# Scans, small VectorE operations and Pool scatters of a gated linear attention, placed elsewhere in a round

## What is computed

```python
h = _layernorm(x) * (1 + ca) + sa                    # x: (32, 256, 128)
q, k, v = h @ W_q, h @ W_k, h @ W_v                  # 16 heads of 64
a = sigmoid(h @ W_gate + b_gate)
def step(S, qkva):                                   # over the 256 tokens
    S = a_t[..., None] * S + k_t[..., None] * v_t[..., None, :]
    return S, einsum('bhk,bhkv->bhv', q_t, S)
x = x + ga * (scan(step) @ W_o)
h = _layernorm(x) * (1 + cb) + sb
probs = sigmoid(h @ router_w.T + routing_bias)       # top 2 of 8, normalised
x = x + gb * (shared(h) + sum over the 2 chosen experts of w_e * down_e(silu(gate_e h) * up_e h))
```

## Time and profile before

| | us |
|---|---|
| median of 3 runs | 1336.66 (1334.47 to 1336.96) |
| the profiled execution's own time | 1335.02 |
| its span, first to last instruction | 1332.9 |
| PE busy | 1209.7 (91%) |
| VectorE busy | 1039.1 (78%) |
| Pool busy | 946.5 (71%) |
| ACT busy | 717.1 (54%) |

### The profile page before, as it was taken

How to read it: one execution, slowest core, us unless ns; L and a number is a source line. 1 busy time by engine, 2 the same in 40 slices (tenths; PEclk the granted TensorE clock), 3 DMA queues, 4 the chain that set the end, 5 groups by cost and what they waited for, 6 DMA issues and landing times. The chain is left out here.

```text
span 1332.9 us, 35442 instructions
## 1 busy us (share of the span) xinstructions
PE 1209.7 (91%) x10935; PEld 1063.2 (80%) x10935; DVE 1039.1 (78%) x2183; ACT 717.1 (54%) x1637; POOL 946.5 (71%) x1288
## 2 busy tenths in 40 slices
PE   5999999999999999998999999999989799999960
PEld 5888878888888878787888888887878688898850
DVE  7778788787878788888878787878766478887767
ACT  4666656556555556555555655655645345445420
POOL 4336687768696968778786969686876457777754
PEclk9999999999999999999999999999999999999995
DMA  8810202021120202020202112020202266666146
GB/s 247 240 69 2 90 22 87 25 85 58 47 98 7 101 8 97 10 95 20 85 24 85 63 42 101 4 101 8 99 26 92 70 189 193 191 178 182 61 155 224
DMA packets 88445, 119.30 MB, mean 90 GB/s; under 512 B 9652, under 2 KB 52327, under 8 KB 88384
## 3 DMA queue, kind: packets, MB, share of 16 engines
q1 hardware_dynamic: 79296, 101.47, 23.7%
q0 software_dynamic: 9088, 17.07, 3.7%
HBM read 50.29 MB, written 61.79 MB: 84 GB/s over the span
## 5 line engine op out<-in xcount | busy, mean ns | idle before, releaser
L1188 DVE TENSOR_TENSOR pairs<-qk_banks,pairs 128x512 f32<-128x512 f32 x256 | 164.5, 684 | 82.0 <-PE qk_banks L1537 81.5
L1638 PE MATMUL vo_bank<-A,shared 128*64 128x256 f32 (+1 forms) x2048 | 197.0, 335 | 27.5 <-POOL A L510 26.7
L710 POOL DMA_INDIRECT y_dram<-pairs,y_row x156 | 158.2, 1014 | 68.2 <-issue 43.9
L1176 DVE TENSOR_TENSOR_SCAN pairs<-pairs,shared 128x515 f32<-128x515 f32 x128 | 174.2, 1361 | 36.3 <-POOL pairs L593 30.1
L510 POOL TENSOR_SCALAR_AFFINE_SELECT A<-A 128x256 f32<-128x256 f32 x256 | 100.0, 416 | 136.3 <-ACT A L786 136.1
L1623 PE MATMUL score_banks<-pairs 64*128 64x128 f32 x2048 | 193.1, 286 | 3.2 <-ACT kx L779 3.2
L1638 PEld LDWEIGHTS vo_bank<-A,shared 128*64 128x64 f32 x2048 | 129.3, 138 | 81.7 <-issue 24.0
L1181 DVE TENSOR_TENSOR_SCAN pairs<-pairs,shared 128x515 f32<-128x515 f32 x128 | 167.8, 1311 | 0.0
L1623 PEld LDWEIGHTS score_banks<-pairs 64*128 64x128 f32 x2048 | 147.0, 189 | 25.7 <-issue 25.7
L584 POOL DMA_INDIRECT rows_dram<-token_rows,dest x120 | 124.9, 1041 | 58.3 <-issue 31.5
L767 ACT ACTIVATE shared<-vo_bank 128x512 f32<-128x512 f32 x128 | 76.5, 598 | 165.0 <-PE vo_bank L1638 165.0
(11 more groups left out here) (252 smaller groups left out, 3163.9 us busy)
## 6 DMA issues: line engine op xcount, KB each, us to landing
rows_dram<-pad_row SPq DMA_DIRECT2D x17, 2112.0 KB, 8.1
ga_all<-rows_dram SPq DMA_DIRECT2D x39, 264.0 KB
pairs<-y_dram SPq DMA_DIRECT2D x16, 512.0 KB
pairs<-in_L_ffn_gate_w_dram SPq DMA_DIRECT2D x39, 128.0 KB
pairs<-in_L_ffn_up_w_dram SPq DMA_DIRECT2D x39, 128.0 KB
ga_all<-in_L_ffn_down_w_dram SPq DMA_DIRECT2D x39, 128.0 KB, 2.2
mod_rows<-mod_rows_dram SPq DMA_DIRECT2D x32, 128.0 KB, 3.1
h_all<-h_tile SPq DMA_DIRECT2D x16, 256.0 KB, 2.3
```

The source lines that it names most:

```text
L710: g.indirect_dma_start(y_dram, bass.IndirectOffsetOnAxis(ap=y_row[:, u, n:n + 1], axis=0), y_out[:, u, n, :], None, bounds_check=TOKENS * ...
L1176: v.tensor_tensor_scan(G[:, 0:WIDE - 1], gi_t[:, 0:WIDE - 1], cap[:, 0:WIDE - 1], 1.0, ALU.mult, ALU.min)
L1188: v.tensor_tensor(out[:, :, :].rearrange("p u (c t) -> p u c t", c=CHUNKS), QKS[:, :, off:off + T].rearrange("p u (c t) -> p u c t", c=CHU ...
L1638: last = t.matmul(VO[h * DK:(h + 1) * DK, u * T + k * P:(u + 1) * T], v_sb[:, k, vcols], blocks.rearrange("p c t -> p (c t)"), start=(k == ...
```

## The change

Five things move, all in the written order. On VectorE the scans of a duo, which stood at the end of a step, now stand in the next step, just ahead of the products that use them. `places` is cut in two: `rank_rows`, which reads the ranks, stands ahead of the scans in step 4, `destinations` behind the products. `choose` goes from step 3 to step 2, the second normalisation is split over steps 5 and 6, `moments` go to steps 1 and 6; what stood ahead of the products (normalisation, `split_h`) now stands behind them. On Pool the eight scatters of a round go from steps 5, 6, 7, 0 in twos to 3, 2, 2, 1 in steps 5, 6, 0, 1, and both `h_rows` stand at the end of their steps.

```diff
--- before.py
+++ after.py
@@ -625,8 +625,8 @@
                     b, d = i * 2 + half, i * 2 * DUOS + s
                     if e == 0 and not (last and half == 1):
                         inverse_std(b + 2)
-                    if s == 0 and three:
-                        scatter_rows(i - 2, s_fill, (i - 2) * 16, (6, 7))
+                    if s < 2 and three:
+                        scatter_rows(i - 2, s_fill, (i - 2) * 16, ((5, 6), (7,))[s])
                     if s in (1, 2) and two:
                         for n in range(2):
                             logits_exp(i - 1, (s - 1) * 2 + n)
@@ -634,17 +634,15 @@
                         update_x(b - 1)
                     if s == 4 and one:
                         inverse_std2(i)
-                    if s == 6 and one:
-                        h_rows((i - 1) * 2 + 1, i - 1, 1, i)
-                    if s >= 5 and two:
-                        scatter_rows(i - 1, s_fill, (i - 1) * 16, ((0, 1), (2, 3), (4, 5))[s - 5])
+                    if s in (5, 6) and two:
+                        scatter_rows(i - 1, s_fill, (i - 1) * 16, ((0, 1, 2), (3, 4))[s - 5])
                     mask_second_head(d)
                     if not (last and s == 2 * DUOS - 1):
                         growth(d + 1)
                     if not (last and s >= 2 * DUOS - 2):
                         gates(d + 2)
-                    if s == 5 and one:
-                        h_rows((i - 1) * 2, i - 1, 0, i)
+                    if s in (5, 6) and one:
+                        h_rows((i - 1) * 2 + s - 5, i - 1, s - 5, i)
 
             inverse_std(1)
             pool.wait_ge(s_wsplit, 4)
@@ -660,7 +658,7 @@
             with pool.Fori(3, ROUNDS - 1) as i:
                 round_of_steps(i, False)
             round_of_steps(ROUNDS - 1, True)
-            scatter_rows(ROUNDS - 2, s_fill, (ROUNDS - 2) * 16, (6, 7))
+            scatter_rows(ROUNDS - 2, s_fill, (ROUNDS - 2) * 16, (5, 6, 7))
             update_x(B - 1)
             logits_exp(ROUNDS - 1, 0)
             inverse_std2(ROUNDS)
@@ -1147,17 +1145,20 @@
                 chosen(k, 6)
                 v.tensor_tensor(picked[:, :, :], pick[:, 0, :, :], pick[:, 1, :, :], ALU.add).then_inc(s_pick, 1)
 
-            def places(k, where=dest):
-
-                def step(count):
-                    alone(s_pl, (k - 1) * 3 + count)
+            def rank_rows(k):
 
                 alone(s_rk, k)
                 v.tensor_tensor(place_e[:, :, :], RANK[:, 0:PT * E].rearrange("p (n e) -> p n e", n=PT),
                                 next_row[:, :].rearrange("p (a e) -> p a e", a=1).broadcast_to([P, PT, E]),
                                 ALU.add).then_inc(s_pl, 1)
-                step(1)
+                alone(s_pl, (k - 1) * 3 + 1)
                 v.tensor_tensor(next_row[:, :], next_row[:, :], RANK[:, PT * E:(PT + 1) * E], ALU.add).then_inc(s_pos, 1)
+
+            def destinations(k, where=dest):
+
+                def step(count):
+                    alone(s_pl, (k - 1) * 3 + count)
+
                 for t in range(TOP):
                     ins = v.tensor_tensor(place_k[:, t, :, :], pick[:, t, :, :], place_e[:, :, :], ALU.mult)
                 ins.then_inc(s_pl, 1)
@@ -1166,6 +1167,10 @@
                 step(3)
                 alone(s_e0, k)
                 v.tensor_copy(where[:, :], place_f[:, :, :].rearrange("p t n -> p (t n)")).then_inc(s_dest, 1)
+
+            def places(k, where=dest):
+                rank_rows(k)
+                destinations(k, where)
 
             def scans(d):
 
@@ -1205,35 +1210,35 @@
                     b, d = i * 2 + half, i * 2 * DUOS + s
                     more = not (last and half == 1)
                     first_head(d)
-                    if s == 3 and two:
-                        choose(i - 1)
-                    if s == 5 and one:
-                        for u in range(2):
-                            normalise2((i - 1) * 2 + u, u, i)
+                    if s == 0 and two:
+                        logits(i - 1)
+                    if s == 4 and two:
+                        rank_rows(i - 1)
+                    if s in (5, 6) and one:
+                        normalise2((i - 1) * 2 + s - 5, s - 5, i)
+                    if not (last and s == 2 * DUOS - 1):
+                        scans(d + 1)
+                        products(d + 1)
+                    if s == 4 and two:
+                        destinations(i - 1)
                     if e == 0 and more:
                         normalise(b * CHUNKS + CHUNKS, s_rs, b + 2, s_xn)
-                    if s == 0 and two:
-                        logits(i - 1)
                     if e == 1 and more:
                         split_h((1 - half) * T, b + 2)
-                    if s == 4 and two:
-                        places(i - 1)
-                    if not (last and s == 2 * DUOS - 1):
-                        products(d + 1)
+                    if s == 2 and two:
+                        choose(i - 1)
                     if s == 3 and two:
                         weigh(i - 2, i - 1)
                     if s == 3 and one:
                         moments2(b - 1, 1, i)
                     if s == 7:
                         moments2(b - 1, 0, i + 1)
-                    if e == (3 if isinstance(b, int) and b == 0 else 2) and not last:
+                    if s == (6 if half else 3 if isinstance(b, int) and b == 0 else 1) and not last:
                         if isinstance(b, int) and b == 0:
                             dve.wait_ge(s_x_rest, 16)
                         moments(b * CHUNKS + 2 * CHUNKS, b + 3)
                     if s == 3 and not one:
                         split_shared_expert()
-                    if not (last and s >= 2 * DUOS - 2):
-                        scans(d + 2)
 
             dve.wait_ge(s_const, 15)
             v.tensor_copy(counting[:, :, :], causal[:, 0:2, :])
@@ -1242,7 +1247,6 @@
             dve.wait_ge(s_sh, 1)
             dve.wait_ge(s_x_next, 16)
             moments(CHUNKS, 2)
-            scans(1)
             for i in range(3):
                 round_of_steps(i, False)
             with dve.Fori(3, ROUNDS - 1) as i:
```

## The result

The changed kernel takes 1345.41 us (median of 6 runs, 1344.34 to 1347.52), the kernel before, on the same chip, 1336.81 (6 runs, 1334.47 to 1340.32): a ratio of 1.0065, 95% interval 1.0049 to 1.0080. It is slower by 8.6, some three times the 2.7 that the prediction took a measurement to tell; 1330.7 had been forecast, with 0.36 on slower.

What follows compares the result with a forecast made beforehand. PE bounds the kernel, busy 57.77 of 61.60 a round. At -0.6 a round, twelve loop rounds give -7.2, rounds 2 and 15 -1.2, rounds 0 and 1 +2.4: -6.0, to 1330.7; range 1296 to 1367.

Steps and rivals of the forecast that it cites:

- A chain exactly as long as PE's work: Each step: scores, first-head masking, scans, products, key copy, next scores take 6.93 against PE's 6.91, so nothing more is hidden.
- A select costs a scan 0.13: Where scans meet Pool's mask: one select lengthens a scan by 0.13, with bounds 0 and 0.39.
- case (i): Mask begun before the first scan: scans lose 0.05 + 0.13, the step is scans' end + 1.74; taken for steps 0, 3, 4.
- The rival of the full hold: Each select costs a scan 0.39, +0.95 a round over 14 rounds, 1355 in all; 12 in 100.
- case (ii): Mask begun in the first scan: scans lose 0.13, step is scans' end + 1.87; taken for steps 2, 6, 7.
- the 8.0 in brackets: Step 1: its length if the second power falls behind a scan, given beside the forecast 7.6.
- case (iii): Mask begun in the second scan: no scan loses, mask ends 0.56 behind, step is scans' end + 2.25; steps 1, 5.
- Step 5, three scatters of 1.40 each, mask near 5.2: Step 5: first scatter 0.92 after the destinations, then 1.40 each, mask near 5.2; step length 8.05, +0.91.
- Rounds 0 and 1, +2.4: Early rounds without routed work or stall to lose: their twelve 6.91 steps become 7.1, +2.4 in all.
- scans and selects do not hinder each other: Rival: step lengths are the larger of chain and PE, -2.6 a round, 1300 in all; 20 in 100.
- the mask behind both scans: Rival: Pool's mask lies behind both scans in every step, +1.75 a round over 14 rounds, 1367; 18 in 100.
- the last rival: PE alone: chain and mask hidden, all 4.2 a round gone, 1278 in all; 5 in 100.

Runs made afterwards that it cites:

- E5: The changed kernel without Pool's causal mask of the second head (its two selects in every step), ScalarE scaling that head's scores by 1e-20; 1291.61, ratio 0.9659.
- E12: The changed kernel with the whole place computation of step 4 ahead of the scans, so destinations come sooner; 1337.56, ratio 1.0003 to the kernel before.
- E6: The changed kernel with the scatters in twos again, in steps 5, 6, 7 and 0; 1338.07, ratio 1.0012 to the kernel before.
- E2: The kernel before with only the scans moved to just ahead of the products, no small work spread; 1439.86, ratio 1.0755.
- E3: The changed kernel with Pool's scatters issued behind the mask, growth and gates of their step; 1430.79, ratio 1.0693 to the kernel before.
- E7: The changed kernel with the scans of step 5 alone run at the end of step 4, three scatters kept; 1340.61, ratio 1.0030 to the kernel before.
- E9: The kernel before with only the place computation split around the products in step 4, scans at the end of the step; 1339.16, ratio 1.0001.
- E10: The kernel before with only DVE's small work spread, Pool's queue as before, scans at the end of the step; 1362.62, ratio 1.0179.
- E11: The kernel before with only Pool's queue as in the changed kernel, DVE as before, scans at the end of the step; 1324.87, ratio 0.9902.

## Why the prediction was wrong

The time lies in the range (1296 to 1367) and on the wrong side. The forecast was -0.6 a round, to 61.0; the loop rounds last 62.17 on average, 0.4 more than before (61.73), and the round that the forecast was read from 0.6 more (62.24 against 61.60). The 1.2 between 61.0 and 62.17, step by step: step 5 +0.82, step 2 +0.28, step 1 +0.14, step 0 +0.10, step 4 +0.05, step 7 -0.18, steps 3 and 6 nothing.

- *Step 4, the stall goes*: right. 7.80 for 7.75, and no wait for `next_row`.
- *A chain exactly as long as PE's work*: the structure right, the size too long. Without selects scans start at 2.70, not 2.83, products follow 0.09 behind the second scan, not 0.2, and the scores 1.65 behind it, not 1.74. That is 2.70 + 2.33 + 1.65 = 6.68: a slack of 0.23 below PE's own 6.91, which is what step 3 of E5 lasts.
- *A select costs a scan 0.13*: right for one select where they alternate (0.13 and 0.16 in step 3), but case (i) charged 0.05 for the other, 0.18 in all. In step 3 the scans end at 5.42 against 5.03 without selects (E5): 0.29 by the two selects, the rest because they start 0.09 later, since `choose` runs into that step. That is 0.2 too little, and the chain was 0.25 too long; that steps 3 and 4 came within 0.05 is luck. The rival of the full hold, 0.39 a select, was not what happened there.
- *Step 2, case (ii), 7.2*: wrong. The mask did not wait inside the first scan. Both selects ran ahead of the scan that had been issued before them, which cost it 0.79 instead of 0.13.
- *Step 1, 7.6*: 7.74. The power that meets the scans pushes the mask to 5.29, behind both, where 4.4 had been taken; the 8.0 in brackets had this case.
- *Step 6, case (ii), 7.8*: the 7.79 is luck. Its second scatter was held too, and the mask began in the second scan, at 5.19, which is case (iii); the scans, at 5.54 instead of 5.92, made up for it.
- *Step 5, three scatters of 1.40 each, mask near 5.2*: the step that failed. It has two errors, and each left the step too short. The destinations were taken to land near the start of the step (5.2 less 4.2 and 0.92); they landed at 0.82, since they stand behind products that the scans make late. And scatters were priced from the earlier trace rows as if nothing could hold them: 1.09, 2.07 and 0.97 with two gaps of 0.30 came to 4.73 in round 8, not 4.2. In those rows they run beside scans too, but are issued where that costs them nothing. The mask starts at 6.47, behind both scans, and the step was costed by the rule for a mask that starts in the second. From there the working holds: mask end at 559.16, attention 0.24 later, next scores 1.45 after that, the 1.69 of the forecast. E12 and E6 bring the step to 7.59 and 7.74.
- *Rounds 0 and 1, +2.4*: +4.0 measured. 1.4 of it is the first step, 9.62 long at a granted clock of 0.68 where the one before had 8.19 at 0.82. Six runs with the scans moved (E2, E3, E5, E6, E7, E12) have 8.40 to 8.44, and E9, which moves none, 9.61, so it varies by execution; the other 2.6 are the forecast's.
- *Rounds 2 and 15, -1.2*: +0.7 (-0.22 and +0.95).
- *The rivals*: that scans and selects do not hinder each other is out by 1.35 for 1.22, and the mask behind both scans came true in two steps of eight, 1 and 5. The 0.82 of step 5 alone is more than the 0.6 that a round was to gain. The 4.2 a round of the last rival does not follow from the earlier trace rows, where 61.60 less 57.77 is 3.83.

What I missed is that the hold-up was priced for selects and, in one row, the residual update, while scatters, and the powers but for the bracket in step 1, were given the length of a place where nothing held them. The Trainium skill (SBUF — State Buffer, section "SBUF: two separate sides") says that of a VectorE instruction with two SBUF inputs and a GpSimd one that reads SBUF, whichever starts first has the shared ports to its end, and the other waits. Of the scan and the scatter issued in it, the rows of E7 agree that the scatter waits; whether its issue reads SBUF no row shows. Of the select, 0.13 lost to some 0.39, the rows do not agree.

## What to carry to other kernels

Before a long VectorE operation with two inputs is moved into a stretch in which Pool works, list everything that Pool has in that stretch, the issuing of its DMAs too, and price each of them as held until that operation ends, unless a row shows it free at just that place. Keep what a late mask waits for short and early; two edits that look like one idea are priced apart, since here one was worth -39 and the other, on top of it, +46. When the order of one engine changes, look at what the other engine's queue has standing behind the first one's result (E10, E3).

## What the runs showed of the hardware

*A scatter issued inside a scan waits for that scan's end and not for the next one's.* The scan ends at 549.71 in E7 and the scatter at 550.61, 0.90 later, which is about its own length, while the second scan runs at its normal 1.20. In step 5 of the changed kernel it ends 0.78 after the first scan's end. The third scatter of E12, issued 0.21 ahead of the scan, took 0.97 and was held in none of twelve rounds. Issued 0.06 ahead, in step 5 of the changed kernel, it was held in seven rounds of twelve (2.06 to 2.08) and not in the other five (0.98 to 1.00).

*The same stall did or did not bring PE's clock down.* In step 4 PE is idle for 1.94 before and 1.93 in E11. Before, the granted clock stays at 1.00 in step 4 of eleven of twelve loop rounds, and the step lasts 9.4 to 9.65; in E11 it falls in eleven of twelve, and in E9, with the same stall, in two. PE in step 4 of round 8, E11, and the granted clock of the second stretch:

```profile
539.21 0.50 PE L1576 MATMUL vo_bank<-big,h_hi 128*128 128x512 f32 x1 [1.93 <-DVE next_row L1158]
...
541.20 2.83 PE L1636 MATMUL vo_bank<-A,shared 128*64 128x256 f32 x16
```

```profile
541.20:543.96 2.76, 2.76 (x18) 1.67 (x17) 2.32 (x3) 0.19 (x1) 2.15 (x3) 0.50 0.15 49
```

PE resumes at a granted clock of 1.00; within 2 us of that it is at the lower level, 1.2 GHz, and the attention product takes 2.83 instead of 1.52. The step lasts 10.90 instead of the 9.40 of the earlier trace rows: 1.5 on top of a stall of 1.9. What makes it fall in one kernel and rarely in the other stays open.
